# Layer 0's output projection: eight row buffers, its weights loaded during the first attention, expert weights asked for behind each step's rows, their halves made between copies

## The reference, cut to what matters

```
xn = layernorm(x)                       # x: 4 x 1024 x 256
s  = L0_attn(xn)                        # ends in  out @ Wo.T + bo
g  = silu(L0_ffn(xn))                   # 8 experts, the best 2 of each token, weighted
x  = x + s * g
xn = layernorm(x)
s  = L1_attn(xn)                        # causal softmax attention, 16 heads
g  = silu(L1_ffn(xn))                   # 16 experts, the best 4, and a shared one
x  = x + s * g
```

## Time and profile before

| | us |
|---|---|
| median of 3 runs | 1841.6 |
| lowest, highest | 1835.0, 1843.37 |
| the profiled execution | 1837.6 |
| its span in the profile | 1835.8 |
| time around the span | 1.8 |
| mean granted TensorE clock, share of full speed | 0.947 |
| PE, DVE, ACT, POOL busy | 1597.9, 1380.6, 1031.0, 667.8 |
| first attention's last store issued | 319.2 |
| f0: first row load issued | 323.3 |
| f0: slot 0 transposed, first up matmul | 379.0, 383.9 |

### The profile page before, as it was taken

How to read it: one execution, slowest core, us unless ns; L and a number is a source line. 1 busy time by engine, 2 the same in 40 slices (tenths; PEclk the granted TensorE clock), 3 DMA queues, 4 the chain that set the end, 5 groups by cost and what they waited for, 6 DMA issues and landing times. The chain is left out here.

```text
span 1835.8 us, 34559 instructions
## 1 busy us (share of the span) xinstructions
PE 1597.9 (87%) x9650; PEld 1238.0 (67%) x9650; DVE 1380.6 (75%) x3710; ACT 1031.0 (56%) x2457; POOL 667.8 (36%) x842
## 2 busy tenths in 40 slices
PE   6996886689954786999999999996899999988896
PEld 5885765579953563554555555544799999977775
DVE  7899998266657877999888888833666666667777
ACT  2664654256656660566676767674556666543443
POOL 2655687400027623111237667620000000056662
PEclk9998999789986995999999999998999999999998
DMA  9333456644435885432435545413864444355552
GB/s 343 130 87 85 106 146 167 205 137 133 133 116 168 290 306 149 99 74 61 106 97 156 160 142 171 128 61 122 274 201 133 133 134 133 117 166 164 169 165 75
DMA packets 279591, 272.72 MB, mean 149 GB/s; under 512 B 121769, under 2 KB 248426, under 8 KB 277356
## 3 DMA queue, kind: packets, MB, share of 16 engines
q1 hardware_dynamic: 255672, 215.41, 39.8%
q0 software_dynamic: 18432, 50.36, 9.0%
q10 hardware_dynamic: 5332, 4.96, 0.8%
HBM read 136.84 MB, written 133.69 MB: 147 GB/s over the span
## 5 line engine op out<-in xcount | busy, mean ns | idle before, releaser
L1890 ACT ACTIVATE ca_PT<-ca_psS 128x512 f32<-128x512 f32 (+3 forms) x768 | 336.3, 494 | 202.9 <-PE ca_psS L1927 197.8
L1430 POOL DMA_INDIRECT g_y<-ys_scratch,pos x128 | 125.0, 977 | 428.2 <-POOLq L73 357.0
L1806 DVE CUSTOM_DVE_ANT_0 ca_masked_row<-ca_psM,mask_row 128x384 f32<-128x384 f32 (+3 forms) x512 | 224.3, 486 | 44.4 <-PE ca_psM L1910 42.4
L1927 PE MATMUL ca_psS<-ca_QS,ca_KS 128*128 128x512 f32 (+1 forms) x480 | 174.7, 367 | 1.4 <-ACT ca_PT L1890 1.4
L1810 DVE TENSOR_REDUCE ca_part<-ca_psM 128x1 f32<-128x512 f32 x256 | 163.4, 685 | 16.1 <-PE ca_psM L1910 14.7
L1939 PE MATMUL ca_psO<-ca_PT,ca_VA 128*17 128x512 f32 (+3 forms) x1536 | 161.0, 491 | 6.0 <-ACT ca_OT L1882 5.9
L1910 PE MATMUL ca_psM<-ca_KS,ca_QS 126*128 126x512 f32 (+2 forms) x480 | 159.0, 379 | 6.5 <-DVE ca_part L1806 4.2
L797 PE MATMUL fa_psO<-fa_weighed,ident 128*128 128x256 f32 x512 | 127.9, 407 | 38.1 <-DVE fa_weighed L585 38.1
L1927 PEld LDWEIGHTS ca_psS<-ca_QS,ca_KS 128*128 128x128 f32 x480 | 90.2, 189 | 86.8 <-ACT ca_PT L1890 58.1
L391 POOL DMA_INDIRECT xs_scratch<-x_sb,pos x128 | 124.6, 973 | 55.9 <-ACT ca_PT L1890 34.1
L797 PEld LDWEIGHTS fa_psO<-fa_weighed,ident 128*128 128x128 f32 x512 | 101.7, 204 | 59.0 <-DVE fa_weighed L585 44.6
(11 more groups left out here) (271 smaller groups left out, 4638.5 us busy)
## 6 DMA issues: line engine op xcount, KB each, us to landing
xs_scratch<-fa_blank SPq DMA_DIRECT2D x32, 640.0 KB, 4.9
x_sb<-xs_scratch SPq DMA_DIRECT2D x143, 128.0 KB, 2.1
ys_scratch<-x_sb SPq DMA_DIRECT2D x143, 128.0 KB, 1.7
xs_scratch<-fa_blank SPq DMA_DIRECT2D x32, 384.0 KB, 6.4
spare<-qk_scratch SPq DMA_DIRECT2D x24, 512.0 KB
ca_QS<-qk_scratch SPq DMA_DIRECT2D x20, 512.0 KB, 6.1
ca_KS<-qk_scratch SPq DMA_DIRECT2D x20, 512.0 KB, 7.6
x_sb<-in_ffn SPq DMA_DIRECT2D x16, 608.0 KB, 4.5
```

The costliest lines, as they stand in the source:

```text
L1430: pool.indirect_dma_start(y[:, t % R, k, :], None, y_dram, bass.IndirectOffsetOnAxis(pos[:, t, k:k + 1], 0)).then_inc(got[t % R], 16)
L1806: ins = dve.tensor_tensor_reduce(masked_row[:, (n * NU + u) % BANKS, h * w:(h + 1) * w], bank[:, h * w:(h + 1) * w], mask_row[:, CHUNK - w ...
L1890: act.activation(PT[:, s % PTS, h, off:CHUNK], psS[(GH * s + h) % BANKS][:, off:CHUNK], ACT.Exp)\
L1927: pe.matmul(psS[tile % BANKS][:, off:CHUNK], KS[slot][:, h, kt * P:(kt + 1) * P], QS[slot][:, h, c * CHUNK + off:(c + 1) * CHUNK], start=T ...
```

## The change

Six edits, all in or around f0:

1. Eight row buffers in place of four (OB0), three raw weight buffers in place of two (RAW).
2. wo and bo are loaded in `first_attention`, in SP's step 23, into tensors of their own; to make room, rot_a and rot_b have one buffer, and POOL waits for its own sum of the tile before.
3. In f0 no raw weights are loaded ahead. They are asked for behind the rows: weights 0, 1, 2 in SP's steps 2, 3, 4, without a wait; weights 3 to 7 in steps 6 to 10, each once the weights three before are split.
4. ACT makes the high half between the second and the third copy of a step.
5. DVE makes the low half one of its steps later, between the second and the third bias add.
6. Scatter j waits for j + 2 transposed tiles in place of j * 4 // 3 + 1.

In layer 1 (f1) `sooner` is 0 and one thing moves: wo and bo are asked for ahead of rows 2 and 3 there.

```diff
@@ first_attention
-        qk, rot_a, rot_b, rot, sq, rotT = (sb(x, [P, 2, NQK]) for x in ("qk", "rot_a", "rot_b", "rot", "sq", "rotT"))
+        qk, rot, sq, rotT = (sb(x, [P, 2, NQK]) for x in ("qk", "rot", "sq", "rotT"))
+        rot_a, rot_b = sb("rot_a", [P, NQK]), sb("rot_b", [P, NQK])
...
+                if n == BESIDE - 1:
+                    sp.dma_start(wo, a["wo0"]).then_inc(wo_in, 16)
+                    sp.dma_start(bo, a["bo0"].partition_broadcast(P)).then_inc(bo_in, 16)
...
+                if t >= 1:
+                    pool.wait_ge(rot_done, t)
...
@@ class Buffers
-    def load(self, sp, o_tile, wo_dram, bo_dram, w_dram):
+    def load(self, sp, o_tile, w_dram, wo_dram=None, bo_dram=None):
         for t in range(self.OB):
+            if t == 2 and wo_dram is not None:
+                sp.dma_start(self.wo, wo_dram).then_inc(self.wo_in, 16)
+                sp.dma_start(self.bo, bo_dram.partition_broadcast(P)).then_inc(self.bo_in, 16)
...
-        sp.dma_start(self.wo, wo_dram).then_inc(self.wo_in, 16)
-        for i in range(self.RAW):
-            sp.dma_start(self.raw[:, i, :], w_dram[i]).then_inc(self.raw_in[i], 16)
-        sp.dma_start(self.bo, bo_dram.partition_broadcast(P)).then_inc(self.bo_in, 16)
+        if not self.SPREAD:
+            for i in range(self.RAW):
+                sp.dma_start(self.raw[:, i, :], w_dram[i]).then_inc(self.raw_in[i], 16)
+class Late(Buffers):
+    RAW = 3
+    SPREAD = True
...
@@ project_beside_experts, SP
-                w = n - LATER
-                if RAW <= w < E:
-                    sp.wait_ge(low_done, w - (RAW - 1))
-                    sp.dma_start(raw[:, w % RAW, :], w_dram[w]).then_inc(raw_in[w % RAW], 16)
+                if not bufs.SPREAD:
+                    refill(n - LATER + sooner)
                 for t in projected(n):
...
+                if bufs.SPREAD:
+                    w = n - OB // PAIR
+                    if 0 <= w < RAW:
+                        sp.dma_start(raw[:, w, :], w_dram[w]).then_inc(raw_in[w], 16)
+                    refill(n - LATER + sooner)
...
@@ POOL
-                    pool.wait_ge(oT_done, j * 4 // 3 + 1)
+                    pool.wait_ge(oT_done, j + 2)
@@ ACT
+                w, todo = n - LATER, projected(n)
+                if not sooner or not todo:
+                    copies(todo)
+                    high_weights(w)
+                else:
+                    copies(todo[:PAIR // 2])
+                    high_weights(w)
+                    copies(todo[PAIR // 2:])
...
@@ DVE
-                for t in projected(n - 1):
+                w, todo = n - LATER - sooner, projected(n - 1)
+                if not sooner or not todo:
+                    add_bias(todo)
+                    low_weights(w)
+                else:
+                    add_bias(todo[:PAIR // 2])
+                    low_weights(w)
+                    add_bias(todo[PAIR // 2:])
...
@@ build
-                    OB0, OT0 = 4, TILES // E0
+                    OB0, OT0 = 8, TILES // E0
```

More of the change, by code:

```diff
@@ L394, in first_attention @@
 def first_attention(nc, a, x_v, x_sb, rows, mean_rstd, xs_dram, logits, w_raw, XT_hi, XT_lo, w_all, bias, cos, sin, rblk, ident,
-                    before, every, tile_ids, o_dram, pos, wts, te, sent):
+                    before, every, tile_ids, o_dram, pos, wts, te, sent, wo, bo, wo_in, bo_in):
     NQ, NQK, NV = HEADS * D, QK_HEADS * D, KV_HEADS * D
@@ L711, in rotate @@
                     pool.wait_ge(rotT_done, t - 1)
-                q3, a3, b3 = (x[:, i % 2, :].rearrange("p (h d) -> p h d", d=D) for x in (qk, rot_a, rot_b))
+                if t >= 1:
+                    pool.wait_ge(rot_done, t)
+                q3, a3, b3 = (x.rearrange("p (h d) -> p h d", d=D) for x in (qk[:, i % 2, :], rot_a[:, :], rot_b[:, :]))
                 cos_i = cos[:, i, :].unsqueeze(1).broadcast_to([P, QK_HEADS, D])
@@ L721, in rotate @@
                 pool.wait_ge(rot_parts, t * 3 + 3)
-                pool.tensor_tensor(rot[:, i % 2, :], rot_a[:, i % 2, :], rot_b[:, i % 2, :], ALU.add).then_inc(rot_done, 1)
+                pool.tensor_tensor(rot[:, i % 2, :], rot_a[:, :], rot_b[:, :], ALU.add).then_inc(rot_done, 1)
             pool.memset(ones[:].bitcast(F32), 1.0).then_inc(ones_done, 1)
@@ L858, in project_beside_experts @@
 def project_beside_experts(nc, tag, o_tile, scale, s_keep, s_dram, w_dram, E, NT, te, w_hi, w_lo, xs_dram, ys_dram, ident, bufs,
-                           load_first=None, load_last=None, lag=2, rows=None, pos=None, sent=None):
+                           load_first=None, load_last=None, lag=2, sooner=0, rows=None, pos=None, sent=None):
     XR, YR, RAW, OB, SB = bufs.XR, bufs.YR, bufs.RAW, bufs.OB, bufs.SB
@@ L940, in beside, with refill @@
                     sp.dma_start(o_st[:, t % OB, :].rearrange("p (g n) -> p g n", g=src.shape[1]), src).then_inc(staged[t % OB], 16)
+                if bufs.SPREAD:
[3 more added lines that the diff above has]
+                    refill(n - LATER + sooner)
+            def refill(w):
+                if RAW <= w < E:
+                    sp.wait_ge(low_done, w - (RAW - 1))
+                    sp.dma_start(raw[:, w % RAW, :], w_dram[w]).then_inc(raw_in[w % RAW], 16)
             if load_first is not None:
@@ L1069, in beside, with copies @@
             def beside(n):
-                for t in projected(n):
+                w, todo = n - LATER, projected(n)
[6 more added lines that the diff above has]
+                    copies(todo[PAIR // 2:])
+                for t in projected(n - 2):
+                    if s_keep is None:
+                        keep(t)
+            def copies(some):
+                for t in some:
                     act.wait_ge(oT_done, t + 1)
@@ L1078, in beside @@
                     act.activation(w_hi[:, w, :], raw[:, w % RAW, :], ACT.Copy).then_inc(hiw_done, 1)
-                for t in projected(n - 2):
-                    if s_keep is None:
-                        keep(t)
             in_steps(act, (LAG, x_high), (LAG + 1, activate), (LAG + 2, h_high), (LAG + 3, take), tiles=NT, first=FIRST, beside=beside)
@@ L1113, in beside, with add_bias @@
             def beside(n):
-                for t in projected(n - 1):
+                w, todo = n - LATER - sooner, projected(n - 1)
[6 more added lines that the diff above has]
+                    add_bias(todo[PAIR // 2:])
+            def add_bias(some):
+                for t in some:
                     dve.wait_ge(s_done, t + 1)
@@ L1739, in load_early @@
                 sp.wait_ge(ao_stored[0], 16 * n)
-                early.load(sp, o_tile, wo_dram, bo_dram, w_dram)
+                early.load(sp, o_tile, w_dram, wo_dram, bo_dram)
             for n in range(SLOTS):
@@ L2043, in build @@
                 xn = s0
+                wo0, bo0 = sb(first, "wo0", [P, KT, HID]), sb(first, "bo0", [P, HID])
+                wo0_in, bo0_in = new_semaphore(nc, top, "wo0_in"), new_semaphore(nc, top, "bo0_in")
                 with ExitStack() as c3:
@@ L2050, in build @@
                         first_attention(nc, a, x_v, x_sb, xn, mean_rstd, xs_dram, logits[:, :, 0:E0], w_raw, XT_hi, XT_lo, w_all, bias_raw, cos, sin, rblk,
[L2051 removed]
+                                        ident, before[:], every[:], tile_ids[:, :], o_dram, pos[0], wts[0], te[0][:, :], sent[0],
+                                        wo0[:, :, :], bo0[:, :], wo0_in, bo0_in)
                 o_rows = o_dram.rearrange("b h s d -> (b h s d)").rearrange("(b t p g n) -> b t p g n", b=BATCH, p=P, g=1, n=HID)
@@ L2059, in build @@
                     w_lo = sb(c2, "ffn0_lo", [P, E0, WE], F32R)
-                    OB0, OT0 = 4, TILES // E0
-                    room = sb(c2, "room0", [P, Buffers.RAW * WE + HID * (KT + 1 + OB0 + OT0 + Buffers.SB + Buffers.XR + Buffers.YR)])
-                    bufs = Buffers(nc, c2, "late", room[:, :], OB0, OT0)
+                    OB0, OT0 = 8, TILES // E0
+                    room = sb(c2, "room0", [P, Late.RAW * WE + HID * (KT + 1 + OB0 + OT0 + Buffers.SB + Buffers.XR + Buffers.YR)])
+                    bufs = Late(nc, c2, "late", room[:, :], OB0, OT0, wo0[:, :, :], bo0[:, :], wo0_in, bo0_in)
                     project_beside_experts(nc, "f0", o_tile0, SHARE, s0, None, a["ffn0"], E0, SLOTS0, te[0], w_hi, w_lo, xs_dram[0],
-                                           ys_dram[0], ident, bufs, lambda sp: bufs.load(sp, o_tile0, a["wo0"], a["bo0"], a["ffn0"]), lag=E0 + 1,
+                                           ys_dram[0], ident, bufs, lambda sp: bufs.load(sp, o_tile0, a["ffn0"]), lag=E0 + 1, sooner=1,
                                            rows=xn, pos=pos[0], sent=sent[0])
```

9 lines of the change are left out of this document (6 added, 3 removed).

## The result

| | kernel before | changed kernel |
|---|---|---|
| runs shown with the profile, median (range) | 1841.2 (1835.0 to 1843.37) | 1821.1 (1815.87 to 1824.24), 4 runs |
| ratio, 95% interval | | 0.9896 (0.9872 to 0.992) |
| profiled execution, span | 1837.6, 1835.8 | 1824.2, 1822.5 |

The forecast was 1824 (1815 to 1833). The kernel became faster by 1.0%, more than the 0.5% that its measurement can tell. The same kernel, run again beside fresh runs of the one before, gave 0.9923 (0.991 to 0.9936) and 0.9905 (0.9888 to 0.9923): by the medians of the three comparisons the gain is 15 to 20 us.

The account below looks back on a forecast made before the run. PE was taken to be held in f0 by row loads queued behind weights, and by later stalls. Gains of 5.8 + 4.8 + 4.7 = 15.3 us gave 1822.3 profiled, 1826.3 off the median; predicted 1824, range 1815 to 1833.

Parts of the forecast that it names:

- row load to tr(4): In f0, from the first row load to the transpose of tile 4: 5.8 us gained.
- tr(4) to tr(28): In f0, from transposing tile 4 to transposing tile 28: 33.6 us becomes 28.8, a gain of 4.8.
- tr(28) to up(4): From transposing tile 28 to the up matmuls of slot 4, through the raw weight refills: gain 4.7 us.
- Opening: Start of f0: row 4, with only rows ahead in SP's queue, lands sooner; gain 5.8 us, bounds from 1.9.
- rival D: Start of f0: something other than the queue held row 4, so only 9.5 us is gained; chance 0.07.
- T7: Time of the transpose of tile 28, start of PE's step 7; to move from 367.84 to 357.3.
- The row behind raw weights 3: Row 28, asked for behind that load, lands at 9.1 us into step 5; PE stalls 0.3 us.
- rival A: Row 28 is late by 2.31 us, the clock falls, landings take 0.9 longer: gain only 8.6 us; chance 0.09.
- Ramp: End of f0, first slots' up matmuls: low weights, then raw weights 5 to 7 landing, set the pace; gain 4.7 us.
- Costs taken as zero: Sooner scatters, wo and bo in the first attention, single rot buffers and layer 1's wo were put at 0 us.
- Rival B: Scatters in f0 become the bound at 2.11 + 0.30 us each, ending at 374.7: gain of 5; chance 0.03.
- Rival C: Rows behind raw weights starve, PE stalls in steps 3, 4, 5 and 7, 7.8 us each: 1853.5; chance 0.03.

Follow-up runs that it names:

- second: The changed kernel run again with no edit: median 1820.7 us, ratio 0.9923 to the kernel before.
- third: The changed kernel run once more with no edit: median 1819.7 us, ratio 0.9905 to the kernel before.
- in place: Changed kernel with raw weights loaded into the low halves' buffers and split there, one per expert: median 1818.5 us, ratio 0.9892 to the kernel before.

## Why the prediction was right

| term, us | before | forecast | measured | gain forecast | gain measured |
|---|---|---|---|---|---|
| row load to tr(4) | 10.9 | 5.2 | 4.5 | 5.8 | 6.4 |
| tr(4) to tr(28) | 33.6 | 28.8 | 27.5 | 4.8 | 6.0 |
| tr(28) to up(4) | 28.0 | 23.3 | 24.3 (22.4 second, 24.0 third) | 4.7 | 3.7 (5.6, 4.0) |
| sum | 72.5 | 57.2 | 56.35 | 15.3 | 16.15 |

Opening: right, and by the cause named. With the queue's order alone undone the same stall arises at tr(8); with that order alone put into the kernel before, 3.85 of its 5.78 us go. That rules out rival D. PE did not even have the gap of 0.31 us that stood ahead of tr(3), so tr(4) came 0.6 sooner than I had it.

tr(4) to tr(28): right, and too careful in three places. One slow tile was left, not two (2.2 us for tr(4) to tr(5), 1.16 to the next). Low weights cost at most 0.12 a piece, and only those of experts 0 and 1 start ahead of tr(28): the prediction counts three, though by its own working low weights 2 end 4.1 us behind T7. The row behind raw weights 3 cost 0.17 and not 0.3; the prediction's own figures, 9.1 against 9.0, give 0.1. That row was the critical place of rival A, and it landed only 0.17 us late. Not foreseen: the rows behind raw weights 0 took up to 7.0 us to land and not 4.6, so the eight buffers had about 1.3 us to spare at tr(12) and not 3.8.

Ramp: the mechanism was right, and two sizes in it were too small. The first is the start of low weights 3: 364.13, or 7.0 us behind tr(28), where the forecast has 6.4. Low weights 4 come behind them, and slot 0's low half behind those, so up(0) came at 10.9 (forecast 10.4), though raw weights 5 had landed at 8.0 as forecast. Raw weights 6 wait for low weights 3, so they were asked for at 365.58 and landed 3.8 us later (I had 3.9), and up(1) came at 14.3 (13.85). The second is the landing of raw weights 7: 373.35 - 367.57 = 5.8 us, beside the slots' loads with the DMA engines fully busy, 1.9 longer than I took and more than the 0.9 that I had set as its bound. In the two other profiles of this kernel it is 5.0 and 5.3. Together they put up(2) at 18.3 and not 17.2 (17.6 and 17.9 in the others), and up(3) at 22.0 and not 20.8. With no landings to wait for (in place), the ramp falls to 20.2.

The clock is in the ramp too. It fell behind the 2.10 us gap and came back shortly before 380. From up(2) to up(3) PE took 3.7 us at the lower clock, for which I had 3.6, and 2.8 in the second profile, where it came back near 377. That makes 1.2 of the 1.9 us by which these two ramps differ; the rest is the landing of raw weights 7. Where the gap is 0.8 us, the clock does not fall and the ramp is 50.5 - 33.2 = 17.3 us.

Costs taken as zero: the first attention shows no lengthening that stands out of 3 us of scatter over thirteen profiles (two of them with the rotation buffers in pairs); scatters are off the path, shown by holding them. One scatter of the changed kernel meets a low half, the one at 350.88 to 352.30, on POOL's timeline after:

```profile
351.31 1.81 POOL L391 DMA_INDIRECT xs_scratch<-s,pos  x1 [0.30 <-issue]
353.44 0.96 POOL L391 DMA_INDIRECT xs_scratch<-s,pos  x1 [0.31 <-issue]
```

It took 1.81 us, the last one 0.96, and nobody waited for it but slot 0's load, which was not the last to be ready. It ended 0.82 us behind the low half. In the thirteen profiles 17 scatters start well inside a low half, and every one of them ends 0.82 to 0.84 us behind its end. 17 more start before a low half and reach into it, like the one at 350.05, and all of these take 0.96. So a scatter loses about what is left of the low half when it starts; the 1.2 us of the prediction, for one that starts 0.15 us into it, is near the most. By the Trainium skill ("SBUF — State Buffer", section "SBUF: two separate sides") a VectorE operation with two inputs in SBUF, as a low half is, holds the shared port pair for its whole length, but only against a GpSimd operation that reads SBUF. The traces agree in that the scatter is held until the low half's end. What the scatter needs the port for is not shown; the lack of descriptors that the prediction names is what the section tells of VectorE's two-port modes.

Rival B would have needed the delay of all 20 scatters. Rival C (stalls in steps 3, 4, 5 and 7) showed nowhere in the changed kernel but for the 0.17 us at tr(28). With four buffers one such stall came, of 2.21 us, and with three raw weights ahead of row 8 one of 3.97, so its mechanism is real; the eight buffers and the spread requests together keep it away. The single rotation buffers were not tried by themselves, nor was the third raw weight buffer, nor the early load of wo and bo; of the last the runs show only that tr(4) comes at 6.4 with wo and bo ahead of row 4 and at 4.9 without, with four buffers in both.

The sum off the median gave 1826.3, and the medians were 1819.7 to 1821.1. f0 as measured gives 16.15 us, 18.1 and 16.2 in the three profiles, of the 15 to 20 between the medians. The rest of the span shows nothing more, and the kernel before itself was profiled only once, so what lies beyond f0's gain is within the scatter of single profiled runs. That the profiled execution took 1824.2 where 1824 was forecast is luck: it was the slowest of its four. And the three terms were off by 0.6, 1.3 and 1.0 us, the last in the other direction, so the sum is nearer than they are.

Two sums of the rivals are off as well. Rival A's gain of 8.6 gives 1829.0 off the profiled execution, and not 1831. Three stalls of rival C give 1845.7, which is 8.1 us slower and not yet the 9.2 that it calls a change; it takes all four.

## What to carry to other kernels

Read the order of requests in a DMA queue as part of the dependency chain: a small load that the bound engine needs next belongs ahead of large ones that are needed late, and moving them was worth 5 us in the kernel before, without any buffer, and 5 to 9 in the changed one. Deeper buffers paid here for what the order still puts ahead of a row, 3 to 5 us. A gap can cost more than its own length: behind one of 2.10 us the clock fell to 1.2 GHz, behind one of 0.80 us it did not. Here the order in which DVE did its work before the first slot made the difference.
